# Plain queries and keys on half the rows each, one slot later, with the output projection behind the weighing

## The chip, the cores and the metric

The kernel runs on one core of one Trainium2 chip. The metric is device time in microseconds (us) of one execution; lower is better. The core has TensorE (PE, with its weight loads PEld), VectorE (DVE), ScalarE (ACT), GpSimd (POOL) and the queue of SyncE (SP), which here only issues transfers. The engines run apart and meet at semaphores.

## The reference

```python
# x: [16 sequences, 256 tokens, 128]; 16 heads of 8; 24 experts of 128 -> 512 -> 128, the best 2 are taken
n = layernorm(x)
ct_q, ct_kv = n @ Wd_q + b, n @ Wd_kv + b             # 64 wide each
query = heads(ct_q @ Wu_q + b) + heads(rope(ct_q @ Wq_r + b))
key   = heads(ct_kv @ Wu_k + b) + heads(rope(n @ Wk_r + b))
value = heads(ct_kv @ Wu_v + b)
x = x + softmax(query @ key.T / 12) @ value @ Wo + b
n = layernorm(x)
scores = n @ gate_w + gate_b;  gates = softmax(top2(scores))
x = x + sum over the two experts of gates * (gelu(n @ w1 + b1) @ w2 + b2)
```

## The kernel before

**Steps and slots.** The attention runs as a pipeline of 16 steps `b`, one for each sequence. Steps 0 to 3 and 12 to 15 are written out, and steps 4 to 11 run in a loop whose waits take their counts from registers. Each step has 16 slots `h`, one for each head. TensorE, ScalarE and VectorE each follow an order written out by hand over `h`; GpSimd and the SP queue follow one over the step. Nothing is reordered at run time: on an engine, an instruction that waits holds up all behind it. After the attention come 88 tiles of expert work (from about 320 us on), which the change does not touch.

**TensorE in a slot.** `pass1` scores a head of a later sequence for its row maxima, `pass2` scores head `h` of this sequence. Between them and the next slot stand small pieces for neighbouring sequences:

- slots 2, 6, 10, 14: `turn_max`, which turns the maxima of four heads into rows, in bank `pa`;
- slot 3: `plain(b + 2, pb)`, the plain parts of queries and keys of sequence `b + 2` (L750 and L751);
- slot 4: `project_out(b - 2, pa)`, the output projection of sequence `b - 2` (L767);
- slot 5 (and 9, 13, 1): `weigh`, the product of four heads' probabilities with their values, in column groups of 32 (L706);
- slot 6, behind `turn_max`: `values(b + 2, pb)` (L755).

`ct` holds the two compressed inputs on top of each other: rows 0 to 63 the queries' and rows 64 to 127 the keys' and values'. The weights of `plain` are padded with zeros on the other 64 rows, so both products run over all 128 rows.

**VectorE in a slot.** It takes the maximum of each `pass1` (L1195), and between these, in order: slot 3 `normalise_out(b - 2)` (L1262) and `best_experts`; slot 4 `take_qk(b + 2, pb)` (L1227), one addition over 512 columns that ends the queries and keys and raises `qk_done`; slot 5 `take_out(b - 2, pa)` (L1268), which adds the projection to `x` and raises `x2_done`; slots 6 and 7 the statistics of the new `x` and the marks of the experts chosen.

**Waits that matter here.**

```python
wait(pe, max_done, m * H + (h - 1))      # pass1: the maximum two heads back must have been taken
wait(pe, spread_in[h // HALF], ...)      # pass1 of heads 0 and 8: rows of queries and keys have landed
wait(pe, x2_done, b - 1)                 # turn_max in slot 6: pa has been read by take_out
wait(pe, mt_done, m * NQ + (j + 1))      # after_turn: ScalarE (take_maxima, L1023) has read pa
wait(pe, qk_done, b + 3)                 # values: pb has been read by take_qk
```

From slot 4 on, `pass1` works on the heads 0, 1, ... of sequence `b + 1`. Their queries and keys go out to memory as bf16 parts and come back spread over partitions: `store_parts`, then `spread_keys` (L452) and `spread_queries` (L461) on the SP queue in the step before. Slot 4 is the first that needs them.

Of the kernel before, what the change touches and what calls it, by code (L numbers as in the profile page):

```python
# [26 lines left out]
ALU = mybir.AluOpType  # L27
# [101 lines left out]
def build(nc, x_in, w_in, r_in, b2_in, w1_in, w2_in, c_in, rows_in, out):  # L129
    with ExitStack() as ctx:  # L130
# [267 lines left out]
        def turns(held, q):  # L398

            return held.attend if q < 2 else held.lead  # L400
# [260 lines left out]
        def _(pe):  # L661
# [10 lines left out]
            def turn_max(b, s, q):  # L672

                m, s, j = turning(b, s, q)
                if q == 0:
                    wait(pe, sc_done, min(b - 2, NB - 2) if isinstance(b, int) else b - 2)
                elif q == 1:
                    wait(pe, x2_done, b - 1)
                elif q == 2:
                    wait(pe, rank_done, b - 1)  # L680
                else:
                    wait(pe, x2T_done, b - 1)
                wait(pe, split_done, m * NQ + (j + 1))
                wait(pe, mt_done, m * NQ + j)
                nc.tensor.matmul(mturn, mxp[j % 2][:, :, :, :].rearrange("p i g t -> p (i g t)"), ident16[:, :],
                                 start=True, stop=True).then_inc(mt_full, 1)
# [62 lines left out]
            def plain(b, bank):  # L749
                nc.tensor.matmul(bank[:, 0:S], wts[:, W_U:W_U + P], ct[:, :], start=True, stop=True)  # L750
                nc.tensor.matmul(bank[:, S:2 * S], wts[:, W_U + 3 * P:W_U + 4 * P], ct[:, :], start=True, stop=True).then_inc(qk_full, 1)  # L751

            def values(b, bank):
                for t in range(QT):
                    mm = nc.tensor.matmul(bank[:, t * P:(t + 1) * P], ct[:, t * P:(t + 1) * P],  # L755
                                          wts[:, W_U + 4 * P:W_U + 5 * P], start=True, stop=True)
                mm.then_inc(v_full, 1)
# [49 lines left out]
            def step(b, s):  # L807
                held = Held(b)
                for h in range(H):
# [4 lines left out]
                    if held.attend:  # L814
                        pass2(b, s, h)
                    if g == 2 and turns(held, q):
                        turn_max(b, s, q)

                    if h == 9 and held.route:
# [14 lines left out]
                    if held.project:  # L834
                        if h == 0:
                            wait(pe, r1_done, b + 3)
                            rotary(b + 2, 1, r2_full, pb)
                        elif h == 3:
                            wait(pe, r2_done, b + 3)
                            plain(b + 2, pb)  # L840
                        elif h == 6:
                            wait(pe, qk_done, b + 3)
                            values(b + 2, pb)
# [6 lines left out]
                            wait(pe, ct_done, b + 4)  # L850
                            rotary(b + 3, 0, r1_full, pb)
                    if held.mix:
                        if h == 4:
                            after_turn(b, 2)
                            project_out(b - 2, pa)
                        elif h == 14 and not held.lead:
                            gate(b - 2, pa)
# [331 lines left out]
        def _(dve):  # L1189
# [30 lines left out]
                nc.vector.tensor_tensor(turn.rearrange("p (i s) -> p i s", i=2), bank[:, :].rearrange("p (i s) -> p i s", i=2),  # L1220
                                        consts[:, None, col:col + S].broadcast_to([P, 2, S]), ALU.mult).then_inc(done, 1)

            def take_qk(b, bank):
                wait(dve, qk_full, b + 1)
                wait(dve, turn_st, b * 2)
                wait(dve, rest_done, b)
                nc.vector.tensor_tensor(qk[:, :], bank[:, :], turn1[:, :], ALU.add).then_inc(qk_done, 1)  # L1227

            def mix(b, bank):

# [204 lines left out]
            def step(b, s):  # L1435
                held = Held(b)
                for h in range(H):
# [11 lines left out]
                    if held.project:  # L1449
                        if h == 1:  # L1450
                            take_rotary(b + 2, r2_full, turn2, C_SIN, r2_done, False, pb)
                        elif h == 4:
                            take_qk(b + 2, pb)
                    if held.prepare and h == 14:
                        take_rotary(b + 3, r1_full, turn1, C_COS, r1_done, True, pb)
                    if held.weigh and h == 10:
# [504 lines left out]
```

## Time and profile before

| | |
|---|---|
| median of 3 runs | 551.39 us (551.08 to 551.43) |
| the profiled execution | 548.95 us, span 547.1 us |
| TensorE busy | 511.3 us, 93% of the span |
| VectorE busy | 387.0 us, 71% |
| ScalarE, GpSimd busy | 337.7 us and 338.0 us, 62% each |
| mean granted TensorE clock | 0.986 of full speed |
| a step of the pipeline, steps 6 to 13 | 18.56 to 18.60 us, from the start of L750 to that of the next step |

The span is that of the instructions; the profiled execution's own time is 1.85 us more. Busy shares are means over stages with different limits, so the stage of the change has to be read by itself.

### The profile page before, as it was taken

To read this page: it belongs to the slowest core of one execution; us is meant where nothing else is said; L and a number is where in the kernel's file an instruction comes from. 1 tells how busy PE (TensorE), PEld (TensorE's weight loads), DVE (VectorE), ACT (ScalarE), POOL (GpSimd) and SP (SyncE) were. 2 spreads that over 40 slices of the span, in tenths; PEclk is the share of its full clock that TensorE was granted. 3 is DMA by queue.
4 is the path that set the end of the run, shared out by engine and by line. 5 is a ranking of instruction groups with operands and counts; after the bars stand their busy time and mean duration, and the time that the engine had idled before them with its cause. 6 is when DMAs were issued, how large, how long until landed. Compare 5 with 4: busy or idle time off the path is not lost.

```text
span 547.1 us, 16858 instructions
## 1 busy us (share of the span) xinstructions
PE 511.3 (93%) x4372; PEld 389.4 (71%) x4373; DVE 387.0 (71%) x1181; ACT 337.7 (62%) x877; POOL 338.0 (62%) x616
## 2 busy tenths in 40 slices
PE   8799989999999999999999986999899999999965
PEld 6565556665666666666666655899899999999932
DVE  7697788888789879878987853767655555555416
ACT  2237767766777777777766764565455555555634
POOL 6746647687777778777877434757665545556510
PEclk9899999999999999999999998999999999999997
DMA  7345675555556555655564276222222222221057
GB/s 245 110 146 151 189 219 159 166 157 168 159 159 194 143 163 172 180 158 163 160 187 148 82 238 229 82 65 61 73 77 63 58 56 62 66 61 46 4 199 262
DMA packets 64977, 74.95 MB, mean 137 GB/s; under 512 B 13666, under 2 KB 50283, under 8 KB 64800
## 3 DMA queue, kind: packets, MB, share of 16 engines
q1 hardware_dynamic: 58976, 63.73, 39.9%
q0 software_dynamic: 4864, 8.54, 4.6%
q10 hardware_dynamic: 1088, 2.10, 1.2%
q8 instruction: 22, 0.36, 0.3%
q14 instruction: 27, 0.22, 0.1%
HBM read 50.96 MB, written 24.54 MB: 138 GB/s over the span
## 4 chain that ended last, share of the span: by engine, by line
PE 61%; DMA 11%; DVE 11%; issue 6%; SPq 4%; POOL 1%; ACT 1%; DVEq 1%; ACTq 0%; POOLq 0%
PE s L965 13%; PE s L973 13%; PE s L668 8%; PE pv L706 7%; PE s L694 4%; DVE mx L1195 3%; DMA few<-weighed_out 2%; PE pb L731 2%; SPq L461 2%; DMA weighed_out<-weighed_sb 2%; PE pb L732 2%; PE pm L694 2%; DMA w<-parts_out 2%; DMA inverse_out<-few 1%; PE pb L726 1%
## 5 line engine op out<-in xcount | busy, mean ns | idle before, releaser
L1195 DVE TENSOR_REDUCE mx<-s 128x2 f32<-128x512 f32 x256 | 170.9, 682 | 46.2 <-PE s L668 42.8
L1170 ACT ACTIVATE pr<-s,wts 128x128 f32<-128x128 f32 x352 | 100.4, 369 | 80.0 <-PE s L965 79.9
L1913 POOL DMA_INDIRECT results<-pr,ridx x88 | 94.8, 1078 | 68.2 <-DVE pr L1370 44.8
L1014 ACT ACTIVATE pr<-s 128x512 f32<-128x512 f32 x176 | 102.4, 593 | 43.1 <-PE s L694 40.3
L668 PE MATMUL s<-w 72*128 72x256 bf16 x512 | 99.3, 275 | 4.6 <-DVE mx L1195 2.2
L973 PE MATMUL s<-w,pr 128*128 x704 | 93.6, 277 | 1.8 <-ACT pr L1170 1.8
L973 PEld LDWEIGHTS s<-w,pr 128*128 128x128 f32 x704 | 86.1, 193 | 2.4 <-issue 2.4
L1801 POOL DMA_INDIRECT dispatched<-pay,pos x64 | 64.7, 1011 | 32.1 <-DVE pos L1343 21.7
L668 PEld LDWEIGHTS s<-w 72*128 72x128 bf16 x512 | 39.2, 100 | 46.9 <-DVE mx L1195 20.6
L706 PE MATMUL pv<-pr,vm 128*32 128x256 f32 x1024 | 68.5, 385 | 0.5 <-ACT pr L1014 0.5
L694 PE MATMUL s<-w 75*128 75x256 bf16 x352 | 67.3, 272 | 0.1
L1014 ACT ACTIVATE pr<-pm 128x512 f32<-128x512 f32 x80 | 47.5, 594 | 32.0 <-PE pm L694 31.8
L965 PE MATMUL s<-work,w1s 128*128 128x128 f32 x352 | 48.5, 282 | 0.5 <-DVE work L1355 0.4
L965 PE MATMUL s<-work,vm 128*128 128x128 f32 x352 | 47.7, 279 | 0.0
L965 PEld LDWEIGHTS s<-work,w1s 128*128 128x128 f32 x352 | 43.8, 196 | 1.2 <-DVE work L1355 1.1
L965 PEld LDWEIGHTS s<-work,vm 128*128 128x128 f32 x352 | 42.8, 192 | 0.1
L706 PEld LDWEIGHTS pv<-pr,vm 128*32 128x32 f32 x1024 | 26.8, 109 | 22.0 <-issue 9.5
L1365 DVE COPY vm<-w 128x640 f32 x44 | 23.9, 543 | 20.6 <-issue 20.2
L1365 DVE COPY w1s<-w 128x640 f32 x44 | 23.0, 522 | 21.8 <-issue 21.8
L694 PEld LDWEIGHTS s<-w 75*128 75x128 bf16 x352 | 33.8, 98 | 5.2 <-DMA w<-mrow 0.3
L1747 POOL CAST mxp<-mx 128x8 bf16<-128x8 f32 x64 | 12.8, 200 | 34.8 <-DVE mx L1195 29.4
L694 PE MATMUL pm<-w 75*128 75x256 bf16 x160 | 30.7, 272 | 1.3 <-DMA w<-mrow 1.2
(238 smaller groups left out, 860.7 us busy)
## 6 DMA issues: line engine op xcount, KB each, us to landing
w<-in_w SPq DMA_DIRECT2D x20, 512.0 KB, 4.7
w<-parts_out SPq DMA_DIRECT2D x32, 288.0 KB
w<-parts_out SPq DMA_DIRECT2D x96, 96.0 KB
parts_out<-qkp SPq DMA_DIRECT2D x16, 384.0 KB
tin<-dispatched SPq DMA_DIRECT2D x88, 66.0 KB
weighed_out<-weighed_sb SPq DMA_DIRECT2D x16, 256.0 KB
w<-results SPq DMA_DIRECT2D x6, 512.0 KB, 8.4
outT<-weighed_out SPq DMA_DIRECT2D x16, 128.0 KB
```

What stands on the lines that cost most here:

```text
L668: mm = nc.tensor.matmul(s1[h % 2][:, t, :], qrows[s][0:KR, h, t * P:(t + 1) * P], krows[s][0:KR, h, :], start=True, stop=True)
L694: mm = nc.tensor.matmul(score_banks[score_bank(h)][:, t, :], krows[s][0:KR + NP, h, t * P:(t + 1) * P], qrows[s][0:KR + NP, h, :], start=T ...
L706: mm = nc.tensor.matmul(pv[VW * c:VW * (c + 1), r, :], vm[s][:, t, (r * NG + c) * 2 + i, :], pr[j % 2][:, c, t, :], start=(i == 0 and t == ...
L965: mm = nc.tensor.matmul(hps[t.pair][:, :, :].rearrange("p a s -> p (a s)")[:, c * P:(c + 1) * P], w1s[t.slot % 4][:, c * P:(c + 1) * P], t ...
L973: mm = nc.tensor.matmul(yps[t.pair][:, 0, 0:D], hT[t.pair][:, c, :], w2[:, bass.ds(e, 1), c, :].rearrange("p o d -> p (o d)"), start=(c == ...
L1014: nc.scalar.activation(pr[h // NG % 2][:, h % NG, :, :], score_banks[score_bank(h)][:, :, :], ACT.Exp, scale=SCALE).then_inc(exp_done, 1)
L1170: last = nc.scalar.activation(hT[t.pair][:, c, :], hps[t.pair][:, :, :].rearrange("p a s -> p (a s)")[:, c * P:(c + 1) * P], ACT.Gelu, bia ...
L1195: nc.vector.tensor_reduce(mx[j % 2][:, g, :], s1[h % 2][:, :, :], AX.X, ALU.max).then_inc(max_done, 1)
L1365: nc.vector.tensor_copy(w1s[t.slot % 4], w1[:, bass.ds(e, 1), :].rearrange("p o f -> p (o f)")).then_inc(w1_done, 1)
L1747: nc.gpsimd.tensor_copy(xp[:, 0, :, :], x).then_inc(split_st, 1)
L1801: nc.gpsimd.indirect_dma_start(dispatched, bass.IndirectOffsetOnAxis(ap=pos[s][:, n:n + 1], axis=0), pay[s][:, t, k, :], None).then_inc(se ...
L1913: nc.gpsimd.indirect_dma_start(results, bass.IndirectOffsetOnAxis(ap=ridx[t.slot][:, 0:1], axis=0), yo[t.slot], None, bounds_check=TOPK * ...
```

## The change

The two products of `plain` become `plain_apart`: each runs over its own 64 rows only (the first in the upper two row groups of TensorE's array, the second in the lower two), and they write to two banks: the queries to `pb`, the keys to `pa`. It stands in slot 4 and not in slot 3, and waits for `after_turn(b, 2)`, since it now writes to `pa`. `project_out` moves from slot 4 to slot 5, behind `weigh`, and waits for `qk_done`. So does `turn_max` of slot 6. `take_qk` becomes two additions over 256 columns, one from each bank.

```diff
+            def plain_apart(b):
+
+                nc.tensor.matmul(pb[:, 0:S], wts[0:DQ, W_U:W_U + P], ct[0:DQ, :], start=True, stop=True)
+                nc.tensor.matmul(pa[:, S:2 * S], wts[DQ:P, W_U + 3 * P:W_U + 4 * P], ct[DQ:P, :], start=True, stop=True).then_inc(qk_full, 1)
...
                     if g == 2 and turns(held, q):
+                        if q == 1 and held.project:
+                            wait(pe, qk_done, b + 3)
                         turn_max(b, s, q)
...
-                        elif h == 3:
+                        elif h == 4:
                             wait(pe, r2_done, b + 3)
-                            plain(b + 2, pb)
+                            after_turn(b, 2)
+                            plain_apart(b + 2)
...
                     if held.mix:
-                        if h == 4:
+                        if h == 5:
                             after_turn(b, 2)
+                            if held.project:
+                                wait(pe, qk_done, b + 3)
                             project_out(b - 2, pa)
...
-            def take_qk(b, bank):
+            def take_qk(b):
                 wait(dve, qk_full, b + 1)
                 wait(dve, turn_st, b * 2)
                 wait(dve, rest_done, b)
-                nc.vector.tensor_tensor(qk[:, :], bank[:, :], turn1[:, :], ALU.add).then_inc(qk_done, 1)
+                nc.vector.tensor_tensor(qk[:, 0:S], pb[:, 0:S], turn1[:, 0:S], ALU.add)
+                nc.vector.tensor_tensor(qk[:, S:2 * S], pa[:, S:2 * S], turn1[:, S:2 * S], ALU.add).then_inc(qk_done, 1)
```

TensorE's order at slots 4 and 5 of a step in the loop, before, from `plain` to the end of `weigh` (L668 is `pass1`, L694 `pass2`, REGISTER_ALU a register operation that can carry a wait):

```order
L750 MATMUL pb<-ct,wts 128x256 [waits r2_done]
L751 MATMUL pb<-ct,wts 128x256
L312 REGISTER_ALU
L312 REGISTER_ALU [waits spread_in0]
L668 MATMUL s_0<-w 128x256 [waits max_done]
...
L694 MATMUL s_1<-w 128x256 [waits exp_done,max_in1]
...
L767 MATMUL pa<-wts,outT 128x128 [waits sc_done,norm_st,mt_done]
...
L668 MATMUL s_1<-w 128x256 [waits max_done]
...
L694 MATMUL pm<-w 128x256 [waits exp_done]
...
L706 MATMUL pv<-pr,vm 32x256 [waits exp_done,pv_done,v_done]
```

The same place after the change (L755 and L756 are the two products, L772 is the output projection, L685 is `turn_max`):

```order
L312 REGISTER_ALU [waits spread_in0]
L668 MATMUL s_0<-w 128x256 [waits max_done]
...
L694 MATMUL s_1<-w 128x256 [waits exp_done,max_in1]
...
L755 MATMUL pb<-ct,wts 128x256 [waits mt_done,r2_done]
L756 MATMUL pa<-ct,wts 128x256
L668 MATMUL s_1<-w 128x256 [waits max_done]
...
L694 MATMUL pm<-w 128x256 [waits exp_done]
...
L706 MATMUL pv<-pr,vm 32x256 [waits exp_done,pv_done,v_done]
...
L772 MATMUL pa<-wts,outT 128x128 [waits norm_st,sc_done,qk_done,mt_done]
...
L668 MATMUL s_0<-w 128x256 [waits max_done]
...
L312 REGISTER_ALU [waits x2_done,qk_done]
L685 MATMUL pa<-ident,mxp 24x128 [waits mt_done,split_done]
```

The first `pass1` that needs `spread_in0` now stands ahead of the plain products, and the projection stands behind eight products of `weigh`, right ahead of slot 6.

VectorE's order at slots 4 and 5 of a step in the loop, from the maximum of slot 4 to `take_out`, before:

```order
L1195 TENSOR_REDUCE mx<-s_0 128x2 [waits split_done]
L312 REGISTER_ALU [waits qk_full]
L1227 TENSOR_TENSOR work<-pb,work 128x512 [waits rest_done,turn_st]
L312 REGISTER_ALU
L1303 CAST argf<-arg 128x4 [waits top_st]
L312 REGISTER_ALU
L1195 TENSOR_REDUCE mx<-s_1 128x2 [waits s1_full]
L1268 ISA [waits xb_done,wo_full]
L1268 TENSOR_TENSOR x_all<-pa,x_all 128x256
```

The same place after the change (L1237 and L1238 are the addition, L1279 is `take_out`):

```order
L1205 TENSOR_REDUCE mx<-s_0 128x2 [waits split_done]
L312 REGISTER_ALU [waits qk_full]
L1237 TENSOR_TENSOR work<-pb,work 128x256 [waits rest_done,turn_st]
L1238 TENSOR_TENSOR work<-pa,work 128x256
L312 REGISTER_ALU
L1314 CAST argf<-arg 128x4 [waits top_st]
L312 REGISTER_ALU
L1205 TENSOR_REDUCE mx<-s_1 128x2 [waits s1_full]
L1279 ISA [waits xb_done,wo_full]
L1279 TENSOR_TENSOR x_all<-pa,x_all 128x256
```

So `take_out` keeps its place on VectorE, while the product that it takes comes a slot and a `weigh` later on TensorE.

## Rows read from the trace of the kernel before

**Rows 1.** The page, busy time, share and instructions of each engine.
```profile
PE 511.3 (93%) x4372; PEld 389.4 (71%) x4373; DVE 387.0 (71%) x1181; ACT 337.7 (62%) x877; POOL 338.0 (62%) x616
```

**Rows 2.** Windows, steps 6 and 7: length, busy per engine (count), clock, DMA, GB/s.
```profile
151.08:169.67 18.59, 18.32 (x168) 11.95 (x167) 15.60 (x43) 13.91 (x33) 14.26 (x32) 1.00 0.59 167
169.67:188.23 18.56, 18.31 (x169) 11.96 (x168) 15.67 (x43) 13.99 (x33) 14.26 (x32) 1.00 0.57 163
```

**Rows 3.** Timeline of TensorE in step 6: start, us to last end, line, count.
```profile
150.86 0.38 PE L694 MATMUL s<-w 75*128 75x256 bf16 x2
151.08 0.60 PE L750 MATMUL pb<-ct,wts 128*128 128x256 f32 x2
...
151.94 0.38 PE L668 MATMUL s<-w 72*128 72x256 bf16 x2
...
152.42 0.68 PE L767 MATMUL pa<-wts,outT 128*128 128x128 f32 x4
152.94 0.38 PE L668 MATMUL s<-w 72*128 72x256 bf16 x2
153.16 0.38 PE L694 MATMUL pm<-w 75*128 75x256 bf16 x2
153.47 1.07 PE L706 MATMUL pv<-pr,vm 128*32 128x256 f32 x16
154.48 0.39 PE L668 MATMUL s<-w 72*128 72x256 bf16 x2
...
155.18 0.22 PE L685 MATMUL pa<-ident,mxp 128*24 128x128 bf16 x1
```

**Rows 4.** Timeline of VectorE in step 6, the same columns.
```profile
150.36 0.69 DVE L1195 TENSOR_REDUCE mx<-s 128x2 f32<-128x512 f32 x1
...
152.66 0.68 DVE L1195 TENSOR_REDUCE mx<-s 128x2 f32<-128x512 f32 x1
153.26 0.68 DVE L1227 TENSOR_TENSOR work<-pb,work 128x512 f32<-128x512 f32 x1
153.86 0.15 DVE L1303 CAST argf<-arg 128x4 f32<-128x4 uint32 x1
153.93 0.68 DVE L1195 TENSOR_REDUCE mx<-s 128x2 f32<-128x512 f32 x1
154.53 0.41 DVE L1268 TENSOR_TENSOR x_all<-pa,x_all 128x256 f32 x1
154.91 0.69 DVE L1195 TENSOR_REDUCE mx<-s 128x2 f32<-128x512 f32 x1
```

**Rows 5.** The chain that ended last, step 6: start, us, what.
```profile
154.61 0.33 DVE x_all L1268
...
156.57 0.65 DVE mx L1195
157.26 0.39 PE s L668 x2
```

**Rows 6.** Timeline of ScalarE in step 6.
```profile
151.53 0.25 ACT L1023 CAST mrow<-pa 24x128 bf16<-24x128 f32 x1
```

**Rows 7.** Timeline of TensorE and its loads, steps 0, 2, 5: `pass1` of slot 4.
```profile
39.23 0.13 PEld L668 LDWEIGHTS s<-w 72*128 72x128 bf16 x2 [0.58 <-DMA w<-parts_out]
...
76.05 0.39 PE L668 MATMUL s<-w 72*128 72x256 bf16 x2 [1.38 <-DMA w<-parts_out]
...
133.78 0.39 PE L668 MATMUL s<-w 72*128 72x256 bf16 x2 [0.38 <-DMA w<-parts_out]
```

**Rows 8.** The chain that ended last, step 5: the transfer that slot 4 waits for.
```profile
129.59 4.06 DMA w<-parts_out
```

**Rows 9.** Windows around the start of L750 in step 7, columns as in rows 2.
```profile
169.60:169.90 0.30, 0.30 (x5) 0.27 (x3) 0.30 (x4) 0.30 (x2) 0.30 (x1) 1.00 1.66 155
169.90:170.20 0.30, 0.30 (x3) 0.27 (x2) 0.30 (x1) 0.30 (x2) 0.30 (x1) 1.00 0.35 56
```

**Rows 10.** Source L750: duration ns min/median/max, first and last start.
```profile
L750 PE MATMUL pb<-ct,wts x28: 377/380/484, 37.9 to 281.3; 128*128 128x256 f32 x28
```

More of the change, by code:

```diff
@@ L1452, in step @@
                         elif h == 4:
-                            take_qk(b + 2, pb)
+                            take_qk(b + 2)
                     if held.prepare and h == 14:
```

## The prediction

> **What bounds the kernel now.** I read the busy shares first. TensorE is busy 93% of the span, the others 62 to 71% [rows 1]. Then the windows by step: in steps 6 and 7 TensorE works 18.32 of 18.59 us and 18.31 of 18.56 us, at full granted clock, against 15.6 on VectorE [rows 2]. That reads like a kernel bound by TensorE, where 0.4 us less in a product is 0.4 us less in a step. The chain that ended last tells more. From slot 2 to slot 9 of such a step it runs through VectorE: `take_out` at 154.61, the maximum from 156.57 to 157.22, and only then back to TensorE's `pass1` at 157.26 [rows 5]. The timelines say why. From 150.36 to at least 155.60 VectorE is never idle: no row carries an idle time, those left out included, and each starts some 0.08 ahead of the end of the one before [rows 4]. It is behind TensorE there: the plain products of 151.08 have been issued by 151.94, but `take_qk` comes to them at 153.26 [rows 3, 4]. `take_out` starts at 154.53, though its product ended at 153.10 (152.42 + 0.68). So two engines share the bound in slots 2 to 9, and what matters is whether the change makes VectorE wait.
>
> All times below count from the start of L750 in step 6, 151.08.
>
> **The products themselves.** Before, both take 151.94 − 151.08 = 0.86 us on TensorE, 0.43 each [rows 3]. Side by side they would take 0.43. The trace has no product on 64 rows; nearest are the products of `weigh`, which lie side by side in four column groups. Sixteen passes of 256 columns in four groups are four rounds of 0.215 (half of 0.43), 0.86 in all. They occupy more: `pass2` ahead of them starts at 153.16 and takes 0.22 (the step from its `pass1`, 152.94), so 153.38 would be free, and the next `pass1` starts at 154.48, 1.10 later [rows 3]. So four go together, and going in and out costs 1.10 − 0.86 = 0.24. For the pair that makes 0.43 + 0.24 = 0.67. Weights of 128 columns, not 32, must load with nothing before to cover them; where L750 had no such cover it lasted 0.484 and not 0.380 [rows 10], so I take **0.70**, a saving of 0.16 a step. Bounds: 0.43 (nothing for going in and out) and 0.86 + 0.24 = 1.10 (not side by side).
> The Trainium skill (TensorEngine Tiling, Theoretical Speedup) gives up to 2x where the contracted side is 64 or less, which would make it 0.43 here, and 14 × 0.43 = 6.0 us off the total if TensorE alone bounded. The four column groups of the trace do reach their factor, less the 0.24 above.
>
> **The move ahead of `pass1`: a transfer loses its cover.** `plain` stood ahead of the first `pass1` that needs `spread_in0`, and hid 0.86 us of the transfer's tail. Now that `pass1` is due at 0.00 and not at 0.86. In steps 0, 2 and 5 it waited even so: 0.58 us for the weights, 1.38 and 0.38 us [rows 7], behind a transfer that took 4.06 us [rows 8]. There `plain` was free. It now comes behind the wait with its whole 0.70. In the other steps the rows show no such wait, so it landed between well before 0.00 and 0.86. In step 7 the DMA share falls from 1.66 to 0.35 at 169.90, 0.23 behind L750 of that step (169.67, the edge of the windows) [rows 2, 9]. I read this as the landing, and take a new wait of 0.3 us (0 to 0.8).
> The plain products also wait for `take_maxima` of slot 3, which ends at 151.53 + 0.25 = +0.70 [rows 6]; `pass1` and `pass2` of slot 4 take 0.44, so that wait and the 0.3 cover each other.
>
> **`take_qk` in two.** 512 columns took 0.60 from start to next start and 0.68 to the end. The nearest row for 256 is `take_out`, 0.38 and 0.41 [rows 4]. So `qk_done` comes at 2.18 + 0.38 + 0.41 = 2.97 and not at 2.86. Bounds: 2.86 (two cost what one did) and 3.1. VectorE doesn't wait for the products here: they end before 2.0 and it arrives at 2.18.
>
> **`project_out` behind `weigh`: the term that decides.** TensorE comes to it at 0.3 + 0.44 + 0.70 + 0.44 + 1.10 = 2.98 at best. It must also wait for `qk_done`, which is queued on VectorE behind all of slots 2 and 3: 2.97, and 3.00 with the 0.03 that such a wait takes. So the 0.16 of the pair is spent in that wait: without it TensorE would come at 3.14. The projection ends 0.71 after its first load (0.68 and 0.03), at 3.71. VectorE is ready for `take_out` at 2.18 + 0.76 + 0.07 + 0.60 = 3.61 (two additions, cast, maximum), and now does wait, up to 3.75. Before it started at 154.53, which is 3.45 [rows 4]. **The step is 0.30 us later here.** All of VectorE's slots 5 to 7 queue behind `take_out`, and the `pass1` at 157.26 behind these; the chain of rows 5 has no slack up to there. TensorE's other way, over `turn_max`, which waits for `x2_done`, moves from 155.18 by the same 0.30 [rows 3]. Bounds: 0.19, if two additions cost what one did (`qk_done` 2.86, projection from 2.89 to 3.60, `take_out` 3.64); and 0.42, if a register operation stands between a wait and the load, as ahead of `turn_max`, which comes 155.18 − 154.94 = 0.24 after `take_out`'s end [rows 3, 4].
>
> **The sum.** Steps 3, 4 and 6 to 13 have both pieces: 10 × 0.30 = 3.0. Steps 0, 2 and 5 lose the cover, 3 × 0.70 = 2.1, less 0.4, since part of what step 4 adds comes off the wait in step 5. Step 1 has no projection and saves 0.16. Where the transfer lands later than 0.3 the arrival at the projection passes 3.00; 0.2 in all for that. 3.0 + 2.1 − 0.4 − 0.16 + 0.2 = **+4.7 us**. The profiled execution took 548.95 us, so the same execution would take 553.7; the median of the runs is 2.4 above it, 551.39, and becomes **556.1**. The tiles of experts behind the attention have no part in it.
>
> **Rivals.** A difference under 0.2% (1.1 us) can't be told from none.
> - *Faster* (0.14). `qk_done` is met early, because VectorE gets to `take_qk` sooner than 2.18. It decides from 0.3 us sooner on: then the projection, `take_out` and VectorE's slots keep their old times, and the pair's saving counts. 14 × 0.16 = 2.2 us less, 549.2; with nothing for going in and out 6.0 less, 545.4. Against it: VectorE is busy without a gap from 150.36 to `take_qk`, and nothing ahead of it is touched.
> - *No change* (0.14). TensorE and VectorE idle 0.27 and 3 us of a step [rows 2], and the 0.30 is taken out of that and not added. Then steps 3 to 13 come out even and steps 0, 1 and 2 give at most 1.2: 551.4 to 552.6. Against it is the chain of rows 5, without a gap between `take_out` and `pass1`.
> - *Slower by much more* (0.11). The pair does not go side by side and pays for going in and out: 1.10. TensorE comes to the projection at 3.38 and not at 3.00, each of ten steps loses 0.68, steps 0, 2 and 5 lose 1.10 and step 1 loses 0.24: 6.8 + 3.3 + 0.2 = 10.3, or 561.7. The four column groups speak against it, though these are columns and these products take rows.
> - *The forecast* (0.61). By the bounds of its terms from 10 × 0.19 + 3 × 0.43 − 0.4 − 0.43 = +2.4 to 10 × 0.42 + 3 × 0.70 − 0.16 + 0.6 (later landings) = +6.7: 553.8 to 558.1.
>
> The range takes in the forecast, no change and most of the way to the slowest case: 550.5 to 560.5. Faster has 0.14, within 0.2% 0.14, slower 0.72.
>
> **What would show it.** Right: two additions of about 0.41 us with a start-to-start of 0.38; L755 and L756 with starts closer than 0.1 us and 0.7 us from the first to the next `pass1`; a wait ahead of L772 for the addition; VectorE idle some 0.1 us ahead of `take_out` for the projection; waits for `w<-parts_out` ahead of the `pass1` of slot 4 in more than five steps; steps 6 to 13 at 18.8 to 18.9 us. Wrong: steps at 18.4 (the pair's saving comes through), `take_qk` ahead of 2.1, or L772 that starts right at the end of `weigh` with `take_out` not waiting.

## The result: slower by 1.7%

The changed kernel takes **563.1 us** in the median of 4 runs (559.6 to 570.2); beside them on the same chip the kernel before took 551.2 in the median of 4. The ratio is 1.0174, with a 95% interval of 1.0116 to 1.0232. The forecast was slower, 556.1, with a range to 560.5. The direction was right and the size was not: by the ratio the change costs 9.6 us, and 4.7 were forecast. Medians in us take in every execution, while all ratios leave out those that are over 1.5% above the fastest of the same kernel beside them. The profiled execution of after took 563.87 us (span 562.0), at a mean granted clock of 0.963 against 0.986.

The page of after, busy time and the granted clock in 40 slices, to be held beside [rows 1]:

```profile
PE 520.2 (93%) x4372; PEld 388.2 (69%) x4373; DVE 386.0 (69%) x1195; ACT 338.1 (60%) x877; POOL 338.0 (60%) x616
...
PEclk8898989999968999999999999699999999999998
```

TensorE has 8.9 us more to do although its products became shorter, and VectorE, ScalarE and GpSimd have what they had. More busy time for the same or less work is what a lower clock would give, and the mean granted clock is lower. The slice with a 6 in the attention lies near 160 us.

Windows of after by step, from `turn_max` in slot 2 to the next: steps 5, 6, 9 and 10, and then step 6 cut in three; columns as in [rows 2].

```profile
136.34:155.99 19.65, 18.24 (x167) 11.47 (x166) 15.54 (x43) 14.12 (x31) 14.27 (x32) 1.00 0.55 156
155.99:181.29 25.30, 24.29 (x167) 14.32 (x166) 15.58 (x43) 14.12 (x31) 14.26 (x32) 0.73 0.44 124
219.92:238.95 19.03, 18.24 (x167) 11.48 (x166) 15.38 (x43) 14.11 (x31) 14.26 (x32) 1.00 0.56 162
238.95:257.97 19.02, 18.25 (x167) 11.48 (x167) 15.40 (x43) 14.02 (x31) 14.28 (x32) 1.00 0.56 161
...
155.99:158.60 2.61, 1.74 (x14) 1.01 (x13) 2.61 (x11) 2.02 (x5) 2.46 (x3) 1.00 0.69 137
158.60:172.30 13.70, 13.62 (x78) 7.72 (x75) 6.59 (x19) 5.65 (x12) 6.27 (x17) 0.50 0.34 105
172.30:181.29 8.99, 8.93 (x80) 5.59 (x78) 6.37 (x14) 6.45 (x15) 5.53 (x13) 1.00 0.51 149
```

Two things are seen. A regular step at full clock takes 19.02 us, 0.45 more than the 18.57 of before, with 0.07 less work on TensorE than in [rows 2] and 0.5 more idle. And in step 6 the granted clock is at the lower of its two levels (1.2 and not 2.4 GHz) for 13.7 us; ahead of that TensorE had worked only 1.74 of 2.61 us, and 0.87 us went to the wait for the transfer. The Trainium skill (TensorE: Matmul & The Clock Gate, Part 1) says that the throttled clock is the engine's default and activity what releases it; a low clock behind a wait, as in these windows, agrees. Two more such stretches of 3.4 us lie in steps 0 (from 42.6) and 2 (from 80.1), each behind waits for the same transfer. Before had none in these steps.

That splits the profiled execution. From step 0 to step 13 before took 243.39 us and after 258.36, so all of the 14.9 us (563.87 − 548.95) lies there. The 20.5 us at half clock cost half of themselves at most, **10.2 us**, if TensorE set the pace all through them. Step 6 says that it is somewhat less: at full clock, with its `pass1` of slot 4 at 1.65 and not at 1.00, it would take some 19.7 us, and it took 25.3, so its 13.7 us cost 5.6 and not 6.8. With that the clock's part is some 9 us (an estimate), and the other **4.7 to 6 us** is what the change does to the steps at full clock.

TensorE's timeline of after in step 10, from slot 4 to `values`, columns as in [rows 3]:

```profile
239.95 0.39 PE L668 MATMUL s<-w 72*128 72x256 bf16 x2 [0.22 <-DMA w<-parts_out]
240.17 0.38 PE L694 MATMUL s<-w 75*128 75x256 bf16 x2
240.49 0.48 PE L755 MATMUL pb<-ct,wts 64*128 64x256 f32 x1
240.49 0.48 PE L756 MATMUL pa<-ct,wts 64*128 64x256 f32 x1
240.81 0.38 PE L755 MATMUL pb<-ct,wts 64*128 64x256 f32 x1
240.81 0.38 PE L756 MATMUL pa<-ct,wts 64*128 64x256 f32 x1
241.12 0.39 PE L668 MATMUL s<-w 72*128 72x256 bf16 x2
...
241.66 1.07 PE L706 MATMUL pv<-pr,vm 128*32 128x256 f32 x16
242.66 0.71 PE L772 MATMUL pa<-wts,outT 128*128 128x128 f32 x4
243.21 0.38 PE L668 MATMUL s<-w 72*128 72x256 bf16 x2
...
244.31 0.22 PE L685 MATMUL pa<-ident,mxp 128*24 128x128 bf16 x1 [0.49 <-DVE x_all L1279]
```

VectorE's timeline of after in step 10, columns as in [rows 4]:

```profile
241.76 0.41 DVE L1237 TENSOR_TENSOR work<-pb,work 128x256 f32<-128x256 f32 x1
242.09 0.41 DVE L1238 TENSOR_TENSOR work<-pa,work 128x256 f32<-128x256 f32 x1
242.43 0.15 DVE L1314 CAST argf<-arg 128x4 f32<-128x4 uint32 x1
242.49 0.68 DVE L1205 TENSOR_REDUCE mx<-s 128x2 f32<-128x512 f32 x1
243.54 0.42 DVE L1279 TENSOR_TENSOR x_all<-pa,x_all 128x256 f32 x1 [0.37 <-issue]
```

The halves do run side by side: each product is two rows of the timeline (fp32 goes through in two passes), and the rows of L755 and L756 start together. From the end of `pass2`'s share, 240.39 (240.17 + 0.22), to the next `pass1` it is 0.73 us; the pair of before took 0.86. Behind that `take_out` waits for the projection, and `turn_max` for `take_out`. Counted from `turn_max` of slot 2 (238.95 in step 10 of after, and 206.22 in step 9 of before, whose step 10 has 4.05 and 4.70 in the second and third row):

| us from `turn_max` of slot 2 | before | after | forecast shift | measured shift |
|---|---|---|---|---|
| first product of the projection | 1.95 | 3.71 | | |
| `take_out` starts | 4.07 | 4.59 | +0.30 | +0.52 |
| `turn_max` of slot 6 | 4.72 | 5.36 | +0.30 | +0.64 |
| the step | 18.57 | 19.02 | +0.30 | +0.45 |

What starts the projection is TensorE's own order, and not the addition. The second addition ends at 242.50, and the projection follows the last product of `weigh` (242.36) by 0.31 us, as the `pass1` behind `weigh` does in before (154.17 and 154.48); and from the start of `weigh` it is 1.00 us, the same as in e2 below, where the projection has no wait for `qk_done`.

The waits of after for the transfer; columns are total us, count, and the longest:

```profile
PE s L668 <- DMA w<-parts_out: 8.0, 10, 2.8
...
PEld s L668 <- DMA w<-parts_out: 7.0, 5, 3.0
```

And the same waits of before:

```profile
PE s L668 <- DMA w<-parts_out: 1.8, 2, 1.4
...
PEld s L668 <- DMA w<-parts_out: 2.5, 3, 1.8
```

The wait for the transfer, whose cover moved away, grew from 4.3 us in five rows to 15.0 us in fifteen. With the load's and the product's wait for one and the same transfer counted once, that is 2.9 us in four steps and 10.2 us in twelve. Most of these waits cost less than they show: in step 10 `pass1` waits 0.22 and starts at 1.00 behind `turn_max`, where before it came at 1.47 behind the plain products.

### The profile page after: what moved, and what is told of

Read it like the earlier page. It is cut to its first block, busy times and chain, and to the rows that moved or that the text cites. A ratio compares the mean times of both kernels' runs of the same rounds, so it can differ in the third digit from the quotient of the medians.

```text
span 562.0 us, 16909 instructions
## 1 busy us (share of the span) xinstructions
PE 520.2 (93%) x4372; PEld 388.2 (69%) x4373; DVE 386.0 (69%) x1195; ACT 338.1 (60%) x877; POOL 338.0 (60%) x616
## 4 chain that ended last, share of the span: by engine, by line
PE 58%; DMA 15%; SPq 7%; DVE 6%; issue 6%; POOL 3%; ACT 1%; DVEq 1%; POOLq 0%; ACTq 0%
PE s L975 13%; PE s L983 12%; PE s L668 7%; PE pv L706 7%; DMA w<-parts_out 5%; PE s L694 3%; SPq L461 2%; DMA weighed_out<-weighed_sb 2%; DMA few<-weighed_out 2%; PE pm L694 2%; DMA parts_out<-qkp 1%; PE pb L760 1%; PE pa L772 1%; DMA w<-results 1%; SPq L452 1%
## 5 line engine op out<-in xcount | busy, mean ns | idle before, releaser
L668 PE MATMUL s<-w 72*128 72x256 bf16 x512 | 101.0, 279 | 10.3 <-DMA w<-parts_out 8.0
L668 PEld LDWEIGHTS s<-w 72*128 72x128 bf16 x512 | 39.0, 101 | 53.2 <-DVE mx L1205 22.7
L706 PE MATMUL pv<-pr,vm 128*32 128x256 f32 x1024 | 72.0, 400 | 1.0 <-ACT pr L1024 1.0
L694 PE MATMUL s<-w 75*128 75x256 bf16 x352 | 68.2, 275 | 0.3 <-DMA w<-mrow 0.3
L706 PEld LDWEIGHTS pv<-pr,vm 128*32 128x32 f32 x1024 | 27.5, 112 | 24.3 <-issue 12.7
L694 PEld LDWEIGHTS s<-w 75*128 75x128 bf16 x352 | 34.1, 99 | 6.1 <-issue 0.6
L1376 DVE COPY vm<-w 128x640 f32 x44 | 23.6, 536 | 20.8 <-issue 20.6
L694 PE MATMUL pm<-w 75*128 75x256 bf16 x160 | 31.6, 279 | 0.5 <-DMA w<-mrow 0.5
```

The lines of the kernel that those rows point to most:

```text
L668: mm = nc.tensor.matmul(s1[h % 2][:, t, :], qrows[s][0:KR, h, t * P:(t + 1) * P], krows[s][0:KR, h, :], start=True, stop=True)
L694: mm = nc.tensor.matmul(score_banks[score_bank(h)][:, t, :], krows[s][0:KR + NP, h, t * P:(t + 1) * P], qrows[s][0:KR + NP, h, :], start=T ...
L706: mm = nc.tensor.matmul(pv[VW * c:VW * (c + 1), r, :], vm[s][:, t, (r * NG + c) * 2 + i, :], pr[j % 2][:, c, t, :], start=(i == 0 and t == ...
L1376: nc.vector.tensor_copy(w1s[t.slot % 4], w1[:, bass.ds(e, 1), :].rearrange("p o f -> p (o f)")).then_inc(w1_done, 1)
```

## The experiments

Ratios are to the kernel before on the same chip at the same time. The chips differ a good deal (the kernel before took 553 us on two of them and 576 to 579 on two others), so times of different groups are not compared, only ratios. "Lost" below is the mean over the runs of time × (1 − mean granted clock), and "rest" is what is left of the time.

### The changed kernel again, on two other chips

No edit. These two carry the question of the clock.

> The changed kernel once more, so that it is timed on the same chip as the three beside it. Both theories: 1.2 to 2.2% over before, with steps 6 to 13 at 19.0 to 19.7 us where the clock is up, and at least one stretch at half clock in steps 0 to 13.

> The changed kernel, timed beside the two others. Both theories: 1.2 to 2.2% over before, mean granted clock 0.005 to 0.015 below that of before.

| | time | ratio | clock | lost | rest | before: clock, lost, rest |
|---|---|---|---|---|---|---|
| first | 587.2 (6 runs) | 1.0185 (1.0123 to 1.0247) | 0.955 | 26.4 | 560.8 | 0.965, 20.3, 555.8 |
| second | 560.4 (5 runs) | 1.0138 (1.0069 to 1.0207) | 0.971 | 16.6 | 545.7 | 0.977, 12.7, 541.1 |

The lower clock comes back on both: 6.1 and 3.9 us more are lost to it, and the rest grows by 5.0 and 4.6 us. The time lost is an upper bound of what the clock costs. In runs of one and the same kernel (13 to 21 runs of before on each of four chips) a us more lost made the run only 0.5 to 0.7 us longer, since a low clock also falls where TensorE is not what is waited for. By that slope the clock's part of the 11.1 and 8.5 us (lost and rest together) is 2.0 to 4.3 us, and 6 to 8 are left.

### Each move alone, and both without the pair

On the kernel before, the plain products a slot later (e1), the projection behind `weigh` (e2), and both (e10):

```diff
-                        elif h == 3:
+                        elif h == 4:              # e1, e10: plain(b + 2, pb)
...
-                        if h == 4:
+                        if h == 5:                # e2, e10: project_out(b - 2, pa)
```

> The kernel before with one edit: the two plain products, whole and in one bank, stand in slot 4 behind its pass1 and pass2. The projection stays in slot 4 behind them. Theory T (the transfer lost its cover): pass1 of slot 4 waits for the spread rows in nearly every step by 0.3 to 0.8 us, steps 6 to 13 take 18.8 to 19.1 us and the total is 4 to 8 us over before, with the granted clock falling in one or more stretches behind the long waits of steps 0 and 2. Theory G (the gate at the projection alone costs the time): no wait of VectorE for the projection arises here, steps stay at 18.6 and the total within 1 us of before.

> The kernel before with one edit: the output projection stands in slot 5 behind the weighing. The plain products stay in slot 3. Theory G: take_out starts 0.4 to 0.6 us later, steps 6 to 13 take 18.9 to 19.1 us, and the total is 4 to 6 us over before, with the clock as before. Theory T: the transfer is covered as before, steps stay at 18.6 and the total within 1 us of before.

> The kernel before with both moves and nothing else: plain products whole, in one bank, in slot 4 behind pass1 and pass2; projection in slot 5 behind the weighing; one addition, no added wait. Alone, the first move left steps 8 to 13 at 18.57 to 18.67 us and the second at 18.58 to 18.65. Theory A (slack): there are some 0.2 us of slack between turn_max of slot 6 and slot 10, and each move uses it up by itself, so together they cost what neither does: TensorE reaches the projection 0.4 us later than with the second move alone, turn_max moves by 0.6 to 0.8, and the steps take 19.0 to 19.3 us. Theory B (the two banks, the split addition or the added waits are what costs): the steps stay at 18.6 to 18.7 us.

e1: 555.7 us, 1.0106 (0.9995 to 1.0218). e2: 550.2 us, 0.9988 (0.993 to 1.0046). e10: 583.4 us, 1.0144 (1.0091 to 1.0197). The window of a regular step of e1:

```profile
194.55:213.14 18.59, 18.24 (x168) 11.94 (x167) 15.34 (x42) 13.81 (x31) 14.28 (x32) 1.00 0.58 166
```

Of e2:

```profile
208.56:227.18 18.62, 18.20 (x168) 12.01 (x167) 15.54 (x42) 14.13 (x31) 14.30 (x32) 1.00 0.58 163
```

And two steps of e10:

```profile
213.26:233.07 19.81, 18.38 (x168) 11.93 (x167) 15.15 (x41) 14.13 (x31) 14.30 (x32) 1.00 0.53 155
233.07:252.19 19.12, 18.38 (x167) 11.94 (x166) 15.26 (x41) 14.07 (x31) 14.54 (x32) 1.00 0.59 163
```

Each move alone leaves the regular step where it was, 18.59 and 18.62, where theory T had 18.8 to 19.1 for e1 and theory G 18.9 to 19.1 for e2; both together make it 19.12 to 19.81. The chip of e10 is one of the longer times, though. The kernel before has no profile there, but e9 below, which hardly differs from it, has: over steps 3 to 12, at full clock in both, e9 takes 190.56 us and e10 195.89, so the two moves cost 0.53 us a step beside it. In the steps of 19.8 us `take_out` starts 1.36 behind the projection's first product and not 0.87; no row tells why, and at full clock such steps show on the chips with the longer times alone. TensorE's timeline of e2 in step 9 shows why the projection's move alone costs nothing:

```profile
208.56 0.23 PE L685 MATMUL pa<-ident,mxp 128*24 128x128 bf16 x1
...
212.00 0.71 PE L767 MATMUL pa<-wts,outT 128*128 128x128 f32 x4
...
213.54 0.22 PE L685 MATMUL pa<-ident,mxp 128*24 128x128 bf16 x1 [0.39 <-DVE x_all L1268]
```

The projection starts at 3.44 and not at 1.95, `take_out` is 0.25 later (212.88, which is 4.32) and `turn_max` is 0.26 later (4.98). The step grows by 0.05. So there are about 0.2 us of slack behind `take_out`, where I had read "no slack". Six kernels on chips of the shorter times give the same figure, each by a regular step beside step 9 of before (`turn_max` of slot 6 at 4.72, 18.57 us):

| | e1 | e2 | e11 | after | e4 | e3 |
|---|---|---|---|---|---|---|
| `turn_max` of slot 6 later by | 0.18 | 0.26 | 0.57 | 0.64 | 0.89 | 0.99 |
| the step longer by | 0.02 | 0.05 | 0.35 | 0.45 | 0.67 | 0.77 |

The step grows by what `turn_max` of slot 6 is late, less 0.2. With both moves the projection starts at 3.92 in the same way (236.99 against the `turn_max` of 233.07), since the plain products now stand ahead of `weigh` and of it, and `take_out` comes 0.72 later.

In e1 the transfer's wait shows by itself: step 5 takes 19.8 us (18.7 in before) and step 2 takes 23.6 (19.9), with 6.8 us at half clock, though nothing else was moved. With 4 runs its ratio can't be told from 1; by its regular steps it is the transfer and the clock alone that would make it slower.

### The pair taken back, and the pair elsewhere

e4 keeps the whole change, but both products run over all 128 rows again (zeros on the other half), so they go one after the other:

```diff
-                nc.tensor.matmul(pb[:, 0:S], wts[0:DQ, W_U:W_U + P], ct[0:DQ, :], start=True, stop=True)
+                nc.tensor.matmul(pb[:, 0:S], wts[:, W_U:W_U + P], ct[:, :], start=True, stop=True)
```

and the same for the second. e3 puts the pair ahead of `pass1` of slot 4, behind `pass2`, so that it can cover the transfer again:

```diff
+                    apart = h == 4 and held.project
+                    if apart:
+                        pass2(b, s, h)
+                        wait(pe, r2_done, b + 3)
+                        after_turn(b, 2)
+                        plain_apart(b + 2)
```

> The changed kernel with the two plain products over all 128 rows as before, still in two banks: the pair side by side is the only part undone. If the pair saves what the trace after says (0.73 from the end of pass2 to the next pass1, against 0.86), TensorE comes 0.1 to 0.2 us later to the projection in each step, and the total is 1 to 3 us over the changed kernel. If going in and out of the half-row form is what costs, it is faster than the changed kernel by 2 us or more.

> The changed kernel, but in slot 4 the order is pass2, the two products on half the rows, pass1. So they lie over the tail of the transfer again. They wait for ScalarE's read of the bank until about +0.7. Theory T: the waits for the spread rows ahead of pass1 shrink to those of before, the clock stays as before, and 5 to 9 us of the 11.9 come back. Theory G: the projection and take_out stay as late as in the changed kernel, so steps 6 to 13 stay at 19.0 and at most 2 us come back (clock apart).

e4: 559.0 us, 1.0147 (1.0031 to 1.0264). e3: 560.8 us, 1.0148 (1.0031 to 1.0266). TensorE's timeline of e4, step 9:

```profile
215.23 0.67 PE L755 MATMUL pb<-ct,wts 128*128 128x256 f32 x2
215.74 0.59 PE L756 MATMUL pa<-ct,wts 128*128 128x256 f32 x2
216.17 0.39 PE L668 MATMUL s<-w 72*128 72x256 bf16 x2
```

In full the products take 0.94 us from the first start to the next `pass1`, against 0.63 for the pair, and regular steps are 19.24 and not 19.02. So the pair is worth 0.2 us a step, all of it inside the lateness that the moves made: it doesn't bring a step back to 18.57. It also shows once more that the addition doesn't start the projection: there the saving would be lost in the wait. e3 pays in the other place. Its `pass2` of slot 4, now the first of the slot, waits for the maxima:

```profile
216.84 0.39 PE L694 MATMUL s<-w 75*128 75x256 bf16 x2 [0.39 <-DMA w<-mrow]
```

That is 1.15 behind `turn_max`. The pair follows at 1.47, `pass1` of slot 4 starts at 2.11 and not at 1.00, and steps are 19.34. The cover is back (one wait for the transfer is left, 0.4 us) and costs more than it hides.

### The second wait, and the addition in two

e5 takes the wait for `qk_done` away from `turn_max` of slot 6 and from `values` where the projection ahead of them has already waited for it. e9 is the kernel before with `take_qk` as two additions over 256 columns of the one bank:

```diff
-                        if q == 1 and held.project:
+                        if q == 1 and held.project and not held.mix:      # e5
...
-                nc.vector.tensor_tensor(qk[:, :], bank[:, :], turn1[:, :], ALU.add).then_inc(qk_done, 1)
+                nc.vector.tensor_tensor(qk[:, 0:S], bank[:, 0:S], turn1[:, 0:S], ALU.add)      # e9
+                nc.vector.tensor_tensor(qk[:, S:2 * S], bank[:, S:2 * S], turn1[:, S:2 * S], ALU.add).then_inc(qk_done, 1)
```

> The changed kernel without the waits for qk_done that turn_max and values of slot 6 repeat: where the projection of slot 5 stands ahead of them on the same engine, it has waited already. In the trace after, turn_max starts 0.32 us behind the end of take_out, against 0.24 before. Theory S (part of the loss is the waits' own register and semaphore operations on TensorE's queue): turn_max starts 0.08 to 0.15 nearer to take_out in the loop steps, these take 18.9 to 19.0 us where no transfer is late, and the total is 0.5 to 1.5 us under the changed kernel, clock apart. Otherwise nothing moves.

> The kernel before with take_qk as two additions over 256 columns, both from the one bank. From the trace after: the two take 0.74 and not 0.68 us to their end. All theories: qk_done 0.06 to 0.1 later, take_out 0.06 later, inside the slack; steps at 18.57 to 18.65 us, total within 1 us of before.

e5: 588.2 us, 1.0133 (1.0062 to 1.0204). e9: 577.8 us, 1.0035 (1.0001 to 1.0069). In e5 `turn_max` follows `take_out`'s end by 0.24 again (239.46 against 238.80 + 0.42), where the changed kernel has 0.35 (244.31 against 243.54 + 0.42):

```profile
238.80 0.42 DVE L1280 TENSOR_TENSOR x_all<-pa,x_all 128x256 f32 x1 [0.30 <-issue]
...
239.46 0.22 PE L685 MATMUL pa<-ident,mxp 128*24 128x128 bf16 x1 [0.39 <-DVE x_all L1280]
```

e2 and e10, which have no second wait either, show 0.24 and 0.25. So the wait costs 0.1 us on TensorE's queue; the total can't tell whether taking it out helps. The two additions by themselves cost at most 0.7%, near the limit of what can be told: they end 0.74 us after the first starts, against 0.68.

### The transfer

Which share is the transfer's? e7 (on the changed kernel) and e8 (on the kernel before) issue the rows that slot 4 needs ahead of the load of the weighed sums on the SP queue. e11 and e12 (changed and before) take the dependence away: from sequence 2 on the transfer of the first eight heads goes to 24 partitions that nothing reads, and `pass1` of slot 4 doesn't wait for it. **They leave out that part of the computation**: heads 0 to 7 of later sequences are scored with the rows of earlier ones, while every transfer and every product is still made.

```diff
-                if held.weigh:
-                    load_weighed(b - 1)
                 ...
                     spread_rows(b + 2, s, 0)
+                if held.weigh:
+                    load_weighed(b - 1)           # e7, e8
...
-                if h % HALF == 0:
-                    wait(pe, spread_in[h // HALF], (m + 1) * SPREAD)
+                if h == 0:
+                    wait(pe, spread_in[0], (min(m, 1) + 1) * SPREAD if isinstance(m, int) else 2 * SPREAD)       # e11, e12
+                elif h == HALF:
+                    wait(pe, spread_in[1], (m + 1) * SPREAD)
...
-                    spread_rows(b + 2, s, 0)
+                    spread_elsewhere(b + 2, s)               # to spread[96:120]
```

> The changed kernel with one swap on the SP queue: the spread of the next rows is issued ahead of the two loads of the weighed sums, so it starts about 1.3 us earlier. Theory T (the transfer without its cover): pass1 of slot 4 no longer waits in steps 6 to 13, these take 19.0 to 19.1 us and none 19.4 or more, the waits of steps 0, 2 and 5 shrink by 1.3 us each, and the median is 3 to 6 us under the changed kernel. If the late projection alone sets the steps, at most 1 us.

> The kernel before with the same swap on the SP queue. Theory T: only steps 0, 2 and 5 wait for the rows (0.6, 1.4 and 0.4 us), and these waits go: 1 to 2.5 us under before. If the later load of the weighed sums holds up normalise_out in slot 3 instead, the steps grow by up to 0.5 us and it is slower.

> The changed kernel, in which the rows of heads 0 to 7 of sequences 2 to 15 are sent as ever, but to memory that nothing reads, and pass1 of slot 4 waits for none of them: these heads are scored with the rows of sequences 0 and 1. Work and traffic stay. Theory T (the transfer whose tail plain used to cover causes most of the loss, by the steps and by the clock that falls behind its waits): TensorE comes to the projection 0.3 us sooner or more, steps 6 to 13 fall from 19.0 to 19.8 us to 18.8 to 18.95, the mean granted clock comes up to that of before, and the median is 5 us or more under the changed kernel beside it. Theory G (the late projection alone): the steps stay at 19.0 or more and at most 2 us come back.

> The kernel before with the same edit (rows of heads 0 to 7 sent elsewhere, pass1 of slot 4 waits for none), as the control. Both theories: plain covers the transfer there but for steps 0, 2 and 5, so the loop steps stay as in before and 0.5 to 3 us come off the total. If it gains 5 us or more, the transfer costs the kernel before as much as the changed one, and theory T falls.

e7: 607.0 us, 1.0396 (1.0297 to 1.0494). e8: 586.7 us, 1.0151 (1.0091 to 1.0212). The order on the queue is not a cure: the weighed sums then come late for `normalise_out`, as this row of e8 shows (2.4 us in one wait in before), and the steps of the loop take 19.2 to 20.0 us in e8 and 20.2 to 26.6 in e7.

```profile
DVE outT L1262 <- DMA sums<-inverse_out: 5.9, 8, 1.4
```

In e7 the waits of `pass1` for the transfer didn't go either, 16.3 us in 15 rows. That trial says nothing on the transfer's price.

e11: 0.9992 (0.9941 to 1.0043), e12: 0.9922 (0.9881 to 0.9963), beside the changed kernel's 1.0138 of the table above, all on one chip. The window of a regular step of e11:

```profile
209.24:228.16 18.92, 18.18 (x167) 11.51 (x166) 15.49 (x43) 14.12 (x31) 14.31 (x32) 1.00 0.58 162
```

And of e12:

```profile
207.19:225.75 18.56, 18.31 (x167) 11.93 (x166) 15.65 (x42) 13.99 (x31) 14.25 (x32) 1.00 0.61 164
```

By these ratios the transfer's waits cost the changed kernel 1.46% and the kernel before 0.78%. The difference, 0.68%, would be the part of the transfer that lost its cover, but the three intervals leave it uncertain by about 0.9% (an estimate, as if they were independent), and it hangs on which executions of e11 are counted: its times run from 548.9 to 587.7 us, and by the medians of all executions the changed kernel has 1.0125, e11 1.0066 and e12 0.9937, which leaves no such difference. The totals don't settle the share.

The profiles say more. In steps 3 to 12 all four kernels ran at full clock; the windows are of before, the changed kernel (the second run of it above), e11 and e12:

```profile
92.96:280.52 187.56, 183.41 (x1662) 119.26 (x1661) 157.77 (x422) 139.19 (x308) 142.87 (x313) 1.00 0.58 167
97.71:290.54 192.83, 182.71 (x1661) 114.88 (x1660) 156.07 (x432) 140.16 (x308) 143.03 (x313) 1.00 0.57 163
94.47:284.92 190.45, 182.43 (x1662) 114.77 (x1661) 156.30 (x432) 140.02 (x308) 143.40 (x313) 1.00 0.59 164
94.53:281.49 186.96, 183.14 (x1662) 119.08 (x1661) 157.72 (x422) 139.01 (x308) 142.88 (x313) 1.00 0.60 168
```

Without the transfer's waits the change costs 190.45 − 186.96 = 3.5 us in these ten steps, which is the projection's lateness: 0.36 us in a regular step (18.92 against 18.56), `take_out` at 4.52 and not 4.07. With them it costs 192.83 − 187.56 = 5.3 us, so the transfer's own part is 1.8 us. These are one execution of each. In a regular step the transfer's wait adds little, since another stands behind it: in e11 the pair waits for ScalarE's reading of `pa`, which it needs because it writes there, and the projection comes only 0.05 sooner than in after (3.66 and 3.71):

```profile
210.71 0.45 PE L771 MATMUL pb<-ct,wts 64*128 64x256 f32 x1 [0.22 <-ACT mrow L1049]
```

### Kept warm over the waits

To test whether idle TensorE is what loses the clock, the changed kernel makes products that nothing reads ahead of `pass1` of slot 4, over the time of its wait; run on two chips:

```diff
+                    if h == 4 and held.project:
+                        wait(pe, r2_done, b + 3)
+                        keep_warm(26 if isinstance(b, int) and b == 0 else 14 if isinstance(b, int) and b == 2 else 4, pb)
```

> The changed kernel with useless products ahead of the pass1 of slot 4 that waits for the spread rows: 26 of them in step 0, 14 in step 2, 4 in the others, 0.11 us each, into a bank that is free there. They use the time of the wait and do no work. Theory C (a large part of the loss is the clock that falls behind these idle times): the granted clock stays up through steps 0 to 13, and the median is 3 to 9 us under the changed kernel, though each step without a late transfer loses up to 0.3 us. If the clock has no part, it is equal or 1 to 3 us slower.

> The changed kernel with the useless products ahead of the pass1 of slot 4, once more beside the changed kernel itself. Theory C (the clock): no step from 2 to 13 at half clock, and the median is 3 us or more under that of the changed kernel. If the clock has no part: equal, or slower.

First 584.2 us, 1.0062 (1.0017 to 1.0107), on the chip where e5, nearly the changed kernel, had 1.0133; then 583.1 us, 1.0123 (1.0065 to 1.0181), where the changed kernel itself had 1.0185. The mean clock was 0.966 and 0.968, against 0.956 and 0.955 for e5 and the changed kernel there. The expectation that no step would fall to half clock was missed: 6.8 us in step 1 of the first run and 10.2 in step 3 of the second did. So useless work makes the changed kernel no slower, and by the middle of the intervals 0.6 to 0.7% faster, though the rest of its time grows from 560.8 to 565.1. The intervals of each pair overlap, so this is a hint and no proof. A low stretch also comes behind another wait, that of `pass2` for the row maxima (TensorE's timeline, step 3 of the second run):

```profile
105.24 0.61 PE L694 MATMUL pm<-w 75*128 75x256 bf16 x2 [1.32 <-DMA w<-mrow]
```

The windows up to that fall and behind it:

```profile
99.00:104.90 5.90, 4.65 (x43) 2.78 (x41) 5.76 (x27) 3.48 (x7) 2.32 (x8) 1.00 0.88 270
104.90:115.10 10.20, 9.86 (x50) 6.08 (x51) 4.29 (x11) 5.12 (x11) 6.04 (x17) 0.50 0.26 70
```

## Why the prediction was right in sign and too small

- **The pair (0.70 forecast): right.** 0.73 us in the trace, side by side. What it is made of was not forecast: it isn't one price for going in and out. The first rows of L755 and L756 start 0.10 behind the end of `pass2`'s share, and that is not of the half rows: in e4 the first product on full rows starts 0.09 behind it (215.23 and 214.92 + 0.22), and in e10, without the wait for ScalarE, 0.01. Each of the two passes then takes 0.32 and 0.31 us, where a pass of 256 columns on its own takes 0.22. The Trainium skill (TensorEngine Tiling (Array Packing), Performance Considerations) says that tiling speeds up TensorE but not the emptying of PSUM. The trace agrees: VectorE's part, which `take_out` queues behind, went from 0.68 to 0.74 us.
- **`take_qk` in two (0.79 to the end): near.** 0.74; the two start 0.33 apart and not 0.38.
- **The gate at the projection, "the term that decides": wrong.** The projection was to wait for `qk_done`, and the pair's saving to be spent in that wait. The addition ends in time (242.50), the projection starts 0.31 behind `weigh` with no wait for it, and the saving does come through, 0.2 us a step by e4. That TensorE's own arrival (2.98 forecast) and the gate (3.00) were priced nearly alike is why the number hardly suffered; that was luck.
- **"The step is 0.30 us later here": too small.** `take_out` starts 0.52 later. The projection is at 3.71 behind `turn_max` and not at 3.61 (its forecast of 3.00 counts from a point 0.61 later), since `pass1` of slot 4 starts 0.09 later than forecast and the pair takes 0.03 more. And `take_out` follows the projection's first product by 0.88 us and not by 0.75: between the projection's end and `take_out` lie 0.17 us in after and e2, where the forecast had 0.04. The upper bound of 0.42 had neither.
- **"`turn_max` moves by the same 0.30": wrong.** By 0.64, since the change also puts a second wait on it (0.1, shown by e5).
- **"The chain has no slack": wrong.** The step grows by 0.2 less than `turn_max` is late, in six kernels. A chain with no gap on VectorE is not a proof, for TensorE's own order can be late by itself; and each move alone fits into the slack, which is why only both together show. So a regular step grew by 0.45 where the sum has 0.30; step 13, which the sum counts with them, by 0.14.
- **The transfer: the step "0.7 in steps 0, 2 and 5, a new wait of 0.3" had the right place.** Steps 7 to 12, all at full clock, lost 3.6 us and not the 2.0 forecast. Steps 0 to 6 lost 1.1 to 2.4 us beside the clock's part, against 2.4. So the sum at full clock was +4.7 to +6 us, against the +4.4 that the forecast had in these steps: near in the sum, and too small in the steps that can be read without the clock.
- **Where it failed: the sum priced nothing for the granted clock.** It was read as 1.00 in steps 6 and 7 of before [rows 2] and carried over unchanged, while the change put waits of 0.9 to 2.8 us ahead of TensorE in steps 0, 2, 5 and 6. In the profiled execution that was some 9 us, 10.2 at most. Over many runs it is less, 2.0 to 6.1 us of 8.5 and 11.1, by the two ways of counting above. The other part, 4.6 to 8 us, is then what the step of 0.30 us, measured at 0.45, and the landings of the transfer made too small.
- **Of the rivals**, faster, no change and "not side by side" are excluded by the timelines and the ratio; the last comes near in its number (561.7) and not by its mechanism. None of them had the clock in it.

Still open is how much of the clock's loss belongs to the change. In steps 0 to 13 the three profiles of the changed kernel have 13.7 to 20.5 us at half clock, but e5, which hardly differs from it, has 3.4; before and e2 have none, e12 has 3.4, and e9, which hardly differs from before, has 10.2 in step 2. The times of the kernel before vary from 546 to 559 us on one chip; and e11, without the transfer's waits, had a median clock of 0.974 against 0.979 in e12. The number of stretches in one profile is chance in part. That the waits cause them is what the order of events in the profiles and the kept-warm runs say, both with the limits given; it is argued and not shown. What makes some chips slower wasn't followed up.

No version beats the kernel before. e2 equals it, e12 isn't a kernel for use, and all with the plain products in slot 4 are slower or can't be told.

## What to carry to other kernels

A piece of work that stands ahead of a late transfer is cover, and moving it costs up to its own length wherever the transfer is late, and perhaps the TensorE clock with it: a forecast for a change that puts new waits ahead of TensorE should carry a term for the clock, or at least say that it has none. Two moves that each fit into a gap can share the same gap; price them together, and test each alone, since that is what shows it. And a product made shorter by row groups pays only where TensorE's own order ends last; here 0.2 us a step came back of the 0.67 that its placement costs with full rows (e4).

## What was not expected of the hardware

- Two fp32 products on 64 rows each, in different row groups and banks, start together in both of their passes, and the next `pass1` starts 0.63 us behind the first of them; on full rows that is 0.86 in before and 0.94 in e4.
- The first product on the full array behind the column groups of `weigh` (the projection in after and e2, `pass1` in before) starts 0.31 us after the last of them; behind the last product of a `pass2`, as the projection in before, it starts 0.15 us after it.
- The stretches at the lower clock in the steps lasted 3.4 to 13.7 us, though the waits ahead of them that the rows show had been 0.9 to 2.8 us.
- One more wait on a count from a register costs TensorE's queue 0.1 us, right ahead of the instruction that it guards.
- The same kernel took 551 to 553 us on some chips and 576 to 579 on others, with a granted clock of 0.98 and 0.96; of these 25 us the clock's loss explains at most 8 to 10.
